# Attention's value product in three bursts instead of four, two heads folded at once by transposes, the end of the program joined to the last experts stage, and a batched comparison in the routing

## The chip, the cores and the metric

The program runs on one core of a Trainium2 chip. The time is that of one execution on the device, in microseconds (us); the median of several executions counts. TensorE (PE) multiplies matrices, VectorE (DVE), ScalarE (ACT) and GpSimd (POOL) work on rows, and SyncE (SP) mostly issues DMA transfers.

## What is computed

Four layers over 4 x 1024 tokens of 256 features, each with a residual and a layer norm: attention with 16 heads of 16 features, a dense mixture of the two best of 8 experts, a wavelet layer with linear attention, and a second mixture with capacity limits. Everything is fp32 at the interface.

```python
scores = jnp.einsum('bhqd,bhkd->bhqk', Q, K) * scale
attn = jax.nn.softmax(scores, axis=-1)
out = jnp.einsum('bhqk,bhkd->bhqd', attn, V)          # 64 heads of 1024 x 1024 in all
x = _layernorm(x + _L0_attn_ref(...)); x = _layernorm(x + _L0_ffn_ref(...))
x = _layernorm(x + _L1_attn_ref(...)); x = _layernorm(x + _L1_ffn_ref(...))
```

## The kernel before

The stages run one after the other, each in a block of its own; between blocks all engines meet, and GpSimd clears the stage's semaphores. Within a block each engine runs its own instruction list in program order, and semaphores order them among each other.

**Attention** (`stage_attention`) goes through the 64 heads (four per loop turn, u = 0 to 3). For each head and each of its 8 key tiles kt (128 keys), TensorE writes the transposed scores (128 keys x 1024 queries, two matmuls, L504) into one of two double banks `ps_scores`; ScalarE writes their exponential into `w` (L538; `w` is the name that the profile has for `c.probs`). The row maxima that the exponential needs are computed two heads ahead: each of 16 units per head is one matmul (L429) into a ring of three PSUM banks `ps_ring`, reduced by VectorE (L552). The ring also carries a small transpose per head (L437, "rows") and the fold. `claim(at)` makes TensorE wait until the bank is free again, that is, until unit at - 3 is used.

The value product (`pv`, L451) multiplies the padded values `v_padded` (32 columns: 16 values, a column of ones for the softmax sum, zeros) with the probabilities. It uses the array as four groups of 32 columns: j = 2 qh + kh, for two halves of the queries and the two key tiles of a pair. So the pair's four matmuls of 512 columns run side by side, and the sums over even and over odd key tiles stay apart in `ps_o`. A head has four such bursts: after key tile 3, 5, 7, and the last one after key tile 1 of the next head. ScalarE copies the bank (L527), and the *fold* (L461) turns it and adds even and odd key tiles by a matmul with a constant `fold`. VectorE then takes the reciprocal of the sum (L574) and multiplies (L576). An fp32 matmul is two instructions in the profile.

**Routing** (`stage_route`, run twice) ends with 64 outer products per run: VectorE makes a one-hot row of 128 (L1103, `e_oh_lo`) and a one-hot of the tile, 156 or 80 wide (L1104, `e_oh_hi`), and TensorE multiplies them (L1128), eight buffers deep.

**The end**: `stage_experts` (the second mixture) adds its rows to `sums` in memory by indirect DMAs of GpSimd (L1187) and waits for them. Then `stage_load_stats` loads `sums` into `y` in eight parts (L763) and takes statistics (L80), `stage_rstd` turns them into scale and shift by a chain of small operations (L789 to L803, the root on ScalarE at L809), and `stage_store` normalises on VectorE (L815) and stores in eight parts (L2065).

Of the kernel before, what the change touches and what calls it, by code (L numbers as in the profile page):

```python
# [19 lines left out]
E = 8  # L20
# [57 lines left out]
def row_stats(nc, c, i):  # L78

    nc.vector.bn_stats(c.six[:, bass.ds(i, 1), :].rearrange("p a d -> p (a d)"),  # L80
                       c.y[:, bass.ds(i, 1), :].rearrange("p a d -> p (a d)"))
# [17 lines left out]
def stage_constants(nc, mem, c):  # L99
# [3 lines left out]
    c.fold = mem.sb("fold", [P, 2 * 32])  # L103
    zeroed, made = mem.sem("consts_zeroed"), mem.sem("consts_made")
    with nc.Block() as block:
        @block.gpsimd
        def _(pool):
            nc.gpsimd.memset(c.ident[:, :], 0.0).then_inc(zeroed, 1)
            nc.gpsimd.memset(c.identb[:, :], 0.0).then_inc(zeroed, 1)
            nc.gpsimd.memset(c.fold[:, :], 0.0).then_inc(zeroed, 1)  # L110

            pool.wait_ge(zeroed, 3)
# [3 lines left out]

            fold = c.fold[:, :].rearrange("p (q r) -> p q r", q=2)
            for kh in range(2):

                pool.wait_ge(made, 2 + kh)  # L120
                nc.gpsimd.affine_select(out=fold, in_=fold, compare_op=ALU.not_equal, fill=1.0, base=-32 * kh,
                                        pattern=[[-64, 2], [-1, 32]], channel_multiplier=1).then_inc(made, 1)
# [142 lines left out]
def stage_attention(nc, a, c):  # L265
# [8 lines left out]
    with ExitStack() as stack:  # L274
# [5 lines left out]
        o_sb = mem.sb("o_transposed", [P, HALF])  # L280
# [5 lines left out]
        rec = mem.sb("o_reciprocal", [P, 2, 4])  # L286
# [17 lines left out]
        FOLD_AT, ROWS_AT = 4, 2  # L304

        def units(first, last, u):

            for kt in range(KT):
# [6 lines left out]
                if kt == FOLD_AT and not (first and u == 0):  # L315
                    yield kt, "fold"
# [10 lines left out]
        PER_GROUP = SLOTS * (2 * KT + 2)  # L327
        assert PER_GROUP % RING == 0

        def count_before(g, first, last, u):  # L330
# [4 lines left out]
            return g * PER_GROUP + (PROLOGUE - 1 + inside)  # L335

        def bank(g, first, last, u, j):
            base = PROLOGUE if first else PROLOGUE - 1
            return ring[(base + sum(len(list(units(first, last, w))) for w in range(u)) + j) % RING]
# [6 lines left out]
        with nc.Block() as block:  # L346
# [38 lines left out]
            def _(pool):  # L385
# [24 lines left out]
                def body(g, first, last):  # L410
                    for u in range(SLOTS):
                        n = g * SLOTS + u

                        wait_apart(pool, spare_p, pv_done, (n - 1) * 4)
# [7 lines left out]
            def _(pe):  # L422
# [18 lines left out]
                def pv(n, u, i):  # L441

                    pe.wait_ge(exp_done, n * KT + 2 * i + 2)
# [4 lines left out]
                    for kh in range(2):  # L448
# [27 lines left out]
                def body(g, first, last):  # L476
                    for u in range(SLOTS):
# [5 lines left out]
                        def emit(kt, kinds):  # L483
                            for j, (step, kind) in todo:
# [5 lines left out]
                                elif kind == "fold":  # L490
                                    fold_unit(n - 1, at, out)
                                else:
                                    max_unit((u + 2) % SLOTS, kt, int(kind[3]), at, out)
                        for kt in range(KT):
# [15 lines left out]
                            if kt == 1 and not (first and u == 0):  # L510
                                pv(n - 1, u + 1, KT // 2 - 1)
# [4 lines left out]
                pv(NH - 1, SLOTS - 1, KT // 2 - 1)  # L516
                end = count_before(GROUPS - 1, False, True, SLOTS)
                fold_unit(NH - 1, end, bank(GROUPS - 1, False, True, SLOTS, 0))

            @block.scalar  # L520
            def _(act):
                def copy_o(n, units_before):

                    act.wait_ge(pv_done, (n + 1) * (KT // 2))

                    act.wait_ge(ring_ready, units_before)
                    nc.scalar.activation(o_sb[:, :], p_o[:, :], ACT.Copy).then_inc(o_copied, 1)  # L527

                def body(g, first, last):
                    for u in range(SLOTS):  # L530
                        n = g * SLOTS + u
                        for kt in range(KT):

                            act.wait_ge(scores_ready, n * KT + kt + 1)
                            if kt % 2 == 0:

                                wait_from(act, pv_done, (n - 1) * (KT // 2) + kt // 2 + 1)
# [1679 lines left out]
```

## Time and profile before

| | us |
|---|---|
| median of 3 runs (range) | 2154.68 (2153.46 to 2157.82) |
| the profiled execution | 2156.69 |
| its span, first to last instruction | 2154.9 |
| TensorE busy | 1854.9 (86%) |
| VectorE busy | 1239.3 (58%) |
| ScalarE busy | 914.2 (42%) |
| GpSimd busy | 438.1 (20%) |

Busy times of a matmul include a modelled end, so neighbours overlap: a step is read from start to start. The granted clock is a share of full speed, 1.00 for 2.4 GHz and 0.50 for 1.2 GHz. "Idle before" names what an engine waited for.

### The profile page before, as it was taken

To read this page: it belongs to the slowest core of one execution; us is meant where nothing else is said; L and a number is where in the kernel's file an instruction comes from. 1 tells how busy PE (TensorE), PEld (TensorE's weight loads), DVE (VectorE), ACT (ScalarE), POOL (GpSimd) and SP (SyncE) were. 2 spreads that over 40 slices of the span, in tenths; PEclk is the share of its full clock that TensorE was granted. 3 is DMA by queue.
4 is the path that set the end of the run, shared out by engine and by line. 5 is a ranking of instruction groups with operands and counts; after the bars stand their busy time and mean duration, and the time that the engine had idled before them with its cause. 6 is when DMAs were issued, how large, how long until landed. Compare 5 with 4: busy or idle time off the path is not lost. (4 is left out here: it accounts for less than half of the span.)

```text
span 2154.9 us, 35159 instructions
## 1 busy us (share of the span) xinstructions
PE 1854.9 (86%) x9600; PEld 1119.4 (52%) x9601; DVE 1239.3 (58%) x2822; ACT 914.2 (42%) x1337; POOL 438.1 (20%) x573
## 2 busy tenths in 40 slices
PE   7899999999999999996599999999994885068771
PEld 4423333333333333363388888888884565037550
DVE  4588888888888888744711111111113796946335
ACT  3336666666666667753022233223331520031330
POOL 2210000000000000030023333333331001202771
PEclk9979999999999999998799999999997998586995
DMA  4511111111111111054433433443442001141224
GB/s 148 182 45 31 30 37 30 30 36 31 30 34 33 30 33 33 16 164 142 159 90 110 111 99 104 115 114 108 97 111 80 1 1 63 63 153 27 46 38 156
DMA packets 103317, 159.34 MB, mean 74 GB/s; under 512 B 20704, under 2 KB 79392, under 8 KB 97760
## 3 DMA queue, kind: packets, MB, share of 16 engines
q1 hardware_dynamic: 69712, 118.46, 16.9%
q0 software_dynamic: 22656, 24.51, 6.5%
q10 hardware_dynamic: 10896, 15.73, 2.1%
q8 instruction: 25, 0.41, 0.1%
q14 instruction: 28, 0.23, 0.0%
HBM read 124.19 MB, written 49.02 MB: 80 GB/s over the span
## 5 line engine op out<-in xcount | busy, mean ns | idle before, releaser
L552 DVE TENSOR_REDUCE unit_max<-ps_ring 128x1 f32<-128x512 f32 x1024 | 655.4, 686 | 83.7 <-PE ps_ring L429 73.4
L538 ACT ACTIVATE w<-ps_scores 128x1024 f32<-128x1024 f32 x512 | 510.0, 1023 | 266.2 <-PE ps_scores L504 254.4
L429 PE MATMUL ps_ring<-k_stack,q_stack 96*128 96x512 bf16 x1024 | 371.7, 391 | 9.8 <-POOL v_padded L392 9.2
L504 PE MATMUL ps_scores<-q_stack,k_stack 98*128 98x512 bf16 x1024 | 305.7, 380 | 0.1
L1495 PE MATMUL m_ps_h<-m_xt,m_w 128*128 128x256 f32 x1248 | 278.0, 381 | 0.8 <-DVE m_xt L1546 0.8
L1507 PE MATMUL m_ps_y<-w,m_ht 128*128 x1248 | 275.8, 379 | 0.0
L451 PE MATMUL ps_o<-w,v_padded 128*32 128x512 f32 x2048 | 272.8, 605 | 0.6 <-ACT w L538 0.6
L429 PEld LDWEIGHTS ps_ring<-k_stack,q_stack 96*128 96x128 bf16 x1024 | 102.1, 100 | 317.3 <-DVE unit_max L552 232.2
L1495 PEld LDWEIGHTS m_ps_h<-m_xt,m_w 128*128 128x128 f32 x1248 | 238.6, 191 | 34.0 <-DVE m_xt L1546 1.2
L1507 PEld LDWEIGHTS m_ps_y<-w,m_ht 128*128 128x128 f32 x1248 | 234.2, 190 | 30.3
L1527 ACT ACTIVATE m_ht<-m_ps_h,m_w 128x256 f32<-128x256 f32 x312 | 131.0, 471 | 143.7 <-PE m_ps_h L1495 143.7
L1546 DVE COPY m_xt<-m_ps_x 128x512 f32<-128x512 f32 x39 | 27.0, 692 | 276.2 <-PE m_ps_x L1483 276.2
L400 POOL TENSOR_SCALAR neg_max<-row_max 128x8 f32<-128x8 f32 x64 | 14.9, 233 | 707.0 <-DVE row_max L560 707.0
L1560 DVE TENSOR_TENSOR m_y<-m_ps_y,biases 128x256 f32<-128x256 f32 x78 | 33.1, 425 | 216.6 <-PE m_ps_y L1507 216.6
L1457 POOL DMA_INDIRECT sums<-m_y,m_is x78 | 124.6, 1597 | 143.9 <-ACT m_y L1532 131.2
L1532 ACT ACTIVATE m_y<-m_y,gains 128x256 f32<-128x256 f32 x78 | 39.6, 508 | 254.7 <-DVE m_y L1560 254.7
L504 PEld LDWEIGHTS ps_scores<-q_stack,k_stack 98*128 98x128 bf16 x1024 | 99.8, 98 | 79.9 <-issue 4.8
L1446 POOL DMA_INDIRECT m_x<-rows,m_ig x78 | 78.2, 1002 | 278.7 <-DVE m_ig L1542 265.8
L451 PEld LDWEIGHTS ps_o<-w,v_padded 128*32 128x32 f32 x2048 | 40.3, 107 | 107.2 <-issue 84.2
L880 PE MATMUL g_ps_t<-ident,g_rows 128*128 128x128 f32 x128 | 22.8, 309 | 79.3 <-DMA g_w<-in_gate 79.3
L1128 PE MATMUL e_ps_map<-e_oh_hi,e_oh_lo 128*128 128x156 f32 (+1 forms) x256 | 58.9, 393 | 22.2 <-DVE e_oh_hi L1104 22.2
L181 PE MATMUL ps_qk<-xt,w_qkv 128*128 128x512 f32 x128 | 58.5, 611 | 17.0 <-DMA bv_all<-in_bv 9.6
(230 smaller groups left out, 2008.9 us busy)
## 6 DMA issues: line engine op xcount, KB each, us to landing
m_w<-in_w SPq DMA_DIRECT2D x39, 1028.0 KB
rows<-g_rows SPq DMA_DIRECT2D x16, 512.0 KB, 2.9
y<-sums SPq DMA_DIRECT2D x16, 512.0 KB, 7.1
q_parts<-qk_part SPq DMA_DIRECT2D x16, 384.0 KB, 3.6
k_parts<-qk_part SPq DMA_DIRECT2D x16, 384.0 KB, 3.8
q_stack<-q_parts SPq DMA_DIRECT2D x64, 96.0 KB
k_stack<-k_parts SPq DMA_DIRECT2D x64, 96.0 KB
xt<-in_xt ACTq DMA_DIRECT2D x8, 512.0 KB, 4.2
```

The source lines that it names most:

```text
L181: mm = nc.tensor.matmul(pq[m][:, :], w[:, k, m * P:(m + 1) * P], xt[u][:, k, :], start=(k == 0), stop=(k == KC - 1))
L429: nc.tensor.matmul(out[:, :], qs[0:STACK, u, qt * P:(qt + 1) * P], ks[0:STACK, u, half * HALF:(half + 1) * HALF], start=True, stop=True).t ...
L451: mm = nc.tensor.matmul(p_o[32 * j:32 * j + 32, :], vpad[u % 2][:, 2 * i + kh, :], pt[:, 2 * i + kh, qh * HALF:(qh + 1) * HALF], start=(i ...
L504: mm = nc.tensor.matmul(p_s[kt % 2][:, half * HALF:(half + 1) * HALF], ks[:, u, kt * P:(kt + 1) * P], qs[:, u, half * HALF:(half + 1) * HALF],
L538: nc.scalar.activation(pt[:, kt, :], p_s[kt % 2][:, :], ACT.Exp, scale=SCALE)\
L552: nc.vector.tensor_reduce(unit_max[:, u % 2, half, qt:qt + 1], src[:, :], axis=AX.X, op=ALU.max).then_inc(ring_used, 1)
L1128: nc.tensor.matmul(p_m[:, 0:2 * tiles], oh_lo[u][:, :], oh_hi[u][:, :, :].rearrange("p a t -> p (a t)"), start=(first and u == 0), stop=(l ...
L1446: pool.indirect_dma_start(out=xg[u][:, j, :], out_offset=None, in_=rows, in_offset=bass.IndirectOffsetOnAxis(ap=ig[u][j][:, :], axis=0))\
L1457: pool.indirect_dma_start(out=sums, out_offset=bass.IndirectOffsetOnAxis(ap=isc[u][j][:, :], axis=0), in_=ys[u][:, j, :], in_offset=None, ...
L1495: mm = nc.tensor.matmul(p_h[f // 2][:, f % 2 * T:(f % 2 + 1) * T], w1s[u][:, at:at + P], xt[u][:, k, :], start=(k == 0), stop=(k == KC - 1))
L1507: mm = nc.tensor.matmul(p_y[j][:, 0:D], ht[u][:, f, j * P:(j + 1) * P], w2[:, bass.ds(e * FC + f, 1), :].rearrange("p a d -> p (a d)"), st ...
L1527: nc.scalar.activation(ht[u][:, f, :], p_h[f // 2][:, f % 2 * T:(f % 2 + 1) * T], func, bias=w1s[u][:, KC * F + f:KC * F + f + 1]).then_in ...
```

## The change

In attention the four column groups now belong to four quarters of the queries (blocks of 128 queries, j of each half), so each key tile makes one group of four matmuls of 256 columns, and all 8 key tiles add up in place. The bursts hold key tiles 0 to 2, 3 to 5 and 6 to 7 and stand after key tile 4, 7, and 1 of the next head. `ps_o` has 256 columns; ScalarE copies them (L527 before) into one half of `o_transposed`, and once in two heads TensorE transposes the four blocks of 128 with the identity. That unit counts as two in the ring ("spare" and "fold") but uses one bank. VectorE's reciprocal and multiply then serve two heads.

In the routing, eight low one-hots are made by one comparison. The end no longer has stages of its own: a new class `Finish` adds its instructions to the lists of the experts stage, in two halves, with the rows shared by ScalarE and VectorE. The constant `fold` is gone.

```diff
-        FOLD_AT, ROWS_AT = 4, 2
+        FOLD_AT, ROWS_AT, COPY_AT = 4, 2, 1
+        EDGES = (0, 3, 6, KT)
+        BURSTS = len(EDGES) - 1
...
-                if kt == FOLD_AT and not (first and u == 0):
+                if kt == FOLD_AT and u % 2 == 0 and not (first and u == 0):
+                    yield kt, "spare"
                     yield kt, "fold"
...
                 def pv(n, u, i):
-                    pe.wait_ge(exp_done, n * KT + 2 * i + 2)
+                    pe.wait_ge(exp_done, n * KT + EDGES[i + 1])
...
-                    for kh in range(2):
-                        for qh in range(2):
-                            j = 2 * qh + kh
-                            mm = nc.tensor.matmul(p_o[32 * j:32 * j + 32, :], vpad[u % 2][:, 2 * i + kh, :],
-                                                  pt[:, 2 * i + kh, qh * HALF:(qh + 1) * HALF],
-                                                  start=(i == 0), stop=(i == KT // 2 - 1))
+                    for kt in range(EDGES[i], EDGES[i + 1]):
+                        probs = pt[:, kt, :].rearrange("p (b j q) -> p j b q", b=2, j=4)
+                        for j in range(4):
+                            mm = nc.tensor.matmul(p_o[32 * j:32 * j + 32, 0:2 * P], vpad[u % 2][:, kt, :],
+                                                  probs[:, j, :, :], start=(kt == 0), stop=(kt == KT - 1))
                     mm.then_inc(pv_done, 1)
...
-                    pe.wait_ge(o_copied, n + 1)
-                    claim(at)
+                    pe.wait_ge(o_copied, n + 2)
+                    claim(at + 1)
                     for blk in range(4):
-                        mm = nc.tensor.matmul(out[:, blk * 64:(blk + 1) * 64], o_sb[:, blk * P:(blk + 1) * P],
-                                              c.fold[:, :], start=True, stop=True)
-                    mm.then_inc(ring_ready, 1)
+                        mm = nc.tensor.transpose(out[:, blk * P:(blk + 1) * P],
+                                                 o_sb[:, blk // 2, blk % 2 * P:(blk % 2 + 1) * P], c.ident[:, :])
+                        if blk >= 2:
+                            mm.then_inc(ring_ready, 1)
...
-                            if kt in (3, 5, 7):
-                                pv(n, u, (kt - 3) // 2)
+                            if kt in (4, 7):
+                                pv(n, u, (kt - 4) // 3)
...
-                        v.tensor_scalar(oh_lo[u][:, :], iota_p[:, :], lo[:, k, bass.ds(i, 1)], None, ALU.is_equal)
+                        if at == 0:
+                            wait_from(dve, mapped, g * (2 * DEEP) + (h - 1) * DEEP)
+                            shape = [P, 2, DEEP // 2, P]
+                            v.tensor_tensor(oh_lo[h][:, :, :, :],
+                                            bcast(iota_p[:, :].unsqueeze(1).unsqueeze(1), shape),
+                                            bcast(lo[:, :, bass.ds(i0, DEEP // 2)].unsqueeze(3), shape), ALU.is_equal)
...
+            if finish is not None:
+                @block.sync
+                def _(sp):
+                    for u in range(2):
+                        sp.wait_ge(added[u], 8 * tiles)
+                    finish.loads_and_stores(sp)
...
+    def statistics(self, dve):
+        for half in range(2):
+            for h in range(4 * half, 4 * half + 4):
+                dve.wait_ge(self.loaded[h], 16)
+                for i in range(h * self.EACH, (h + 1) * self.EACH):
+                    last = row_stats(nc, c, i)
...
+        for h in (4, 5):
+            for i in range(h * self.EACH, (h + 1) * self.EACH):
+                last = normalised(nc, c, self.rows[:, i, :], i)
+            last.then_inc(self.dve_rows, 1)
+    def roots_and_rows(self, act):
+        for half in range(2):
+            act.wait_ge(self.var_ready, half + 1)
+            nc.scalar.activation(self.root[:, cut], self.var[:, cut], ACT.Sqrt).then_inc(self.root_ready, 1)
+            act.wait_ge(self.scale_ready, half + 1)
+            for h in ((0, 1, 2, 3), (6, 7))[half]:
+                for i in range(h * self.EACH, (h + 1) * self.EACH):
+                    last = nc.scalar.activation(self.rows[:, i, :], c.y[:, i, :], ACT.Identity,
+                                                scale=c.rstd[:, i:i + 1], bias=c.nmr[:, i:i + 1])
+                last.then_inc(self.act_rows, 1)
```

On TensorE, around the fold in the loop over heads, the list before reads as follows (`ps_o` marks a burst of the value product, `ps_ring` with stacks a maximum, with `o_transposed` the fold; the count is that of matmuls as written, each fp32 one being two instructions):

```order
L429 MATMUL ps_ring<-k_stack,q_stack 128x512
L451 MATMUL ps_o<-w,v_padded 32x512 x4
L429 MATMUL ps_ring<-k_stack,q_stack 128x512
L504 MATMUL ps_scores<-q_stack,k_stack 128x512 x2
L429 MATMUL ps_ring<-k_stack,q_stack 128x512
L461 MATMUL ps_ring<-fold,o_transposed 128x64 x4
L429 MATMUL ps_ring<-k_stack,q_stack 128x512
L504 MATMUL ps_scores<-q_stack,k_stack 128x512 x2
L429 MATMUL ps_ring<-k_stack,q_stack 128x512
L451 MATMUL ps_o<-w,v_padded 32x512 x4
```

and the list of the changed kernel at the same place, once in two heads:

```order
L423 MATMUL ps_ring<-k_stack,q_stack 128x512
L445 MATMUL ps_o<-w,v_padded 32x256 x12
L454 MATMUL ps_ring<-ident,o_transposed 128x128 x4
L423 MATMUL ps_ring<-k_stack,q_stack 128x512
L500 MATMUL ps_scores<-q_stack,k_stack 128x512 x2
L423 MATMUL ps_ring<-k_stack,q_stack 128x512 x2
L500 MATMUL ps_scores<-q_stack,k_stack 128x512 x2
L423 MATMUL ps_ring<-k_stack,q_stack 128x512 x2
L500 MATMUL ps_scores<-q_stack,k_stack 128x512 x2
L423 MATMUL ps_ring<-k_stack,q_stack 128x512
L445 MATMUL ps_o<-w,v_padded 32x256 x12
```

The fold has moved from the middle of a stretch between two bursts to right behind a burst, and three key tiles instead of two stand between the bursts. On ScalarE, at the end of the program, the list before ends with the root:

```order
L1299 ACTIVATE m_y_1<-m_y_1,gains 128x256 x2
L1169 UNCONDITIONAL_BRANCH
L806 UNCONDITIONAL_BRANCH
L809 ACT_TABLE_LOAD
L809 ACTIVATE r_root<-r_var 128x32
```

and that of the changed kernel has rows behind each of two roots:

```order
L1313 ACTIVATE m_y_1<-m_y_1,gains 128x256 x2
L2141 ACT_TABLE_LOAD
L2141 ACTIVATE f_root<-f_var 128x16
L2146 ACTIVATE f_rows<-y,nmr,rstd 128x256 x16
L2141 ACTIVATE f_root<-f_var 128x16
L2146 ACTIVATE f_rows<-y,nmr,rstd 128x256 x8
```

The second root stands behind 16 rows, and the branches from block to block are gone.

## Rows read from the trace of the kernel before

**Rows 1.** Timeline of GpSimd at the start: start, duration, engine, line, operation, count.

```profile
2.17 0.63 POOL L121 TENSOR_SCALAR_AFFINE_SELECT fold<-fold 128x64 f32<-128x64 f32 x2
```

**Rows 2.** Table of stretches: stretch, length, busy of each engine, granted clock, DMA share.

```profile
200.00:800.00 600.00, 600.00 (x3508) 211.81 (x3504) 526.32 (x961) 411.44 (x433) 44.05 (x192) 1.00 0.11 32
```

**Rows 3.** Timeline of TensorE over one head.

```profile
501.06 1.00 PE L461 MATMUL ps_ring<-fold,o_transposed 128*128 128x64 f32 x8
501.90 0.38 PE L429 MATMUL ps_ring<-k_stack,q_stack 96*128 96x512 bf16 x1
502.12 0.59 PE L504 MATMUL ps_scores<-q_stack,k_stack 98*128 98x512 bf16 x2
502.55 0.38 PE L429 MATMUL ps_ring<-k_stack,q_stack 96*128 96x512 bf16 x1
502.86 1.07 PE L451 MATMUL ps_o<-w,v_padded 128*32 128x512 f32 x8
503.86 0.39 PE L429 MATMUL ps_ring<-k_stack,q_stack 96*128 96x512 bf16 x1
...
513.56 1.00 PE L461 MATMUL ps_ring<-fold,o_transposed 128*128 128x64 f32 x8
```

**Rows 4.** The first four matmuls of that burst, its loads, and durations min/median/max (ns).

```profile
502.86 0.64 PE L451 MATMUL ps_o<-w,v_padded 128*32 128x512 f32 x4
502.86 0.16 PEld L451 LDWEIGHTS ps_o<-w,v_padded 128*32 128x32 f32 x8 [0.42 <-issue]
L451 PE MATMUL ps_o<-w,v_padded x2048: 589/593/617, 137.4 to 925.7; 128*32 128x512 f32 x187
```

**Rows 5.** Waits from 200 to 800 us: total, times, longest.

```profile
DVE unit_max L552 <- PE ps_ring L429: 49.6, 144, 0.5
```

**Rows 6.** Timeline of VectorE in the same head.

```profile
502.10 0.21 DVE L574 RECIPROCAL o_reciprocal<-ps_ring 128x8 f32<-128x8 f32 x1
...
502.66 1.28 DVE L552 TENSOR_REDUCE unit_max<-ps_ring 128x1 f32<-128x512 f32 x2
504.29 2.54 DVE L552 TENSOR_REDUCE unit_max<-ps_ring 128x1 f32<-128x512 f32 x4 [0.35 <-PE ps_ring L429]
```

**Rows 7.** Timeline of TensorE in the first experts stage.

```profile
1244.49 1.46 PE L1495 MATMUL m_ps_h<-m_xt,m_w 128*128 128x256 f32 x6
1245.78 0.60 PE L1483 MATMUL m_ps_x<-ident,m_x 128*128 128x128 f32 x4
```

**Rows 8.** Routing: VectorE's timeline, the second routing's stretch, a group of VectorE.

```profile
1060.41 0.27 DVE L1103 TENSOR_SCALAR e_oh_lo<-e_iota_p,e_lo 128x128 f32<-128x128 f32 x1
1060.61 0.37 DVE L1104 SCALAR_TENSOR_TENSOR e_oh_hi<-e_iota_t,e_hi,e_value 128x156 f32<-128x156 f32 x1
...
1941.00:1968.50 27.50, 27.27 (x128) 27.28 (x128) 25.90 (x127) 0.00 (x0) 0.00 (x0) 0.50 0.00 1
...
L1041 DVE TENSOR_TENSOR e_pr<-e_ex,e_rc 128x256 f32<-128x256 f32 x2 | 0.8, 425 | 0.1
```

**Rows 9.** The end: GpSimd's drain and clears, a ScalarE group, the timeline.

```profile
L1169 POOLq DRAIN  x1: 3937/3937/3937, 2115.6 to 2115.6; - x1
L46 POOLq EVENT_SEMAPHORE_RANGE_CLEAR  x31: 37/38/43, 2119.8 to 2140.8; - x31
L1299 ACT ACTIVATE m_y<-m_y,gains 128x256 f32<-128x256 f32 x40 | 20.3, 508 | 74.0 <-DVE m_y L1367 69.6 <-issue 4.3
2119.80 7.86 SPq L763 DMA_DIRECT2D y<-sums  x8
2127.47 5.54 DVE L80 BATCH_NORM_STATS2 six<-y 128x6 f32<-128x256 f32 x16 [1.14 <-DMA y<-sums]
...
2136.80 0.21 DVE L789 TENSOR_TENSOR mean<-six 128x32 f32<-128x32 f32 x1 [0.30 <-PEq L759]
...
2140.73 10.43 DVE L815 TENSOR_SCALAR s_rows<-y,rstd,nmr 128x256 f32<-128x256 f32 x32 [0.56 <-PEq L784]
2142.14 9.42 SPq L2065 DMA_DIRECT2D out_rows<-s_rows  x8
```

More of the change, by code:

```diff
@@ L109, in _ @@
             nc.gpsimd.memset(c.identb[:, :], 0.0).then_inc(zeroed, 1)
-            nc.gpsimd.memset(c.fold[:, :], 0.0).then_inc(zeroed, 1)
-            pool.wait_ge(zeroed, 3)
+            pool.wait_ge(zeroed, 2)
             for m in (c.ident, c.identb):
@@ L534, in body @@
                             act.wait_ge(scores_ready, n * KT + kt + 1)
[L535 to L537 removed]
+                            if kt in EDGES:
+                                wait_from(act, pv_done, (n - 1) * BURSTS + EDGES.index(kt) + 1)
                             nc.scalar.activation(pt[:, kt, :], p_s[kt % 2][:, :], ACT.Exp, scale=SCALE)\
                                 .then_inc(exp_done, 1)
[L540 to L541 removed]
+                            if kt == COPY_AT and not (first and u == 0):
+                                copy_o(n - 1, u + 1, count_before(g, first, last, u))
                 groups(act, body)
[L543 removed]
+                copy_o(NH - 1, SLOTS - 1, count_before(GROUPS - 1, False, True, SLOTS))
             @block.vector
@@ L604, in _ @@
                 end = count_before(GROUPS - 1, False, True, SLOTS)
-                normalise(NH - 1, end, bank(GROUPS - 1, False, True, SLOTS, 0))
+                normalise(NH - 2, NH // 2 - 1, end, bank(GROUPS - 1, False, True, SLOTS, 1))
         mem.clear()
@@ L972, in stage_route @@
         ownf = mem.sb("e_ownf", [P, owners])
-        oh_lo = [mem.sb(f"e_oh_lo{u}", [P, P]) for u in range(DEEP)]
-        oh_hi = [mem.sb(f"e_oh_hi{u}", [P, 2, tiles]) for u in range(DEEP)]
+        oh_lo = [mem.sb(f"e_oh_lo{h}", [P, 2, DEEP // 2, P]) for h in range(2)]
+        oh_hi = [mem.sb(f"e_oh_hi{u}", [P, 2, tiles]) for u in range(2 * DEEP)]
         table = mem.sb("e_table", [P, 2, tiles])
@@ L1125, in outer_products, with stage_experts @@
                 def outer_products(g, first, last):
-                    for u in range(DEEP):
-                        pe.wait_ge(hi_done, g * DEEP + u + 1)
-                        nc.tensor.matmul(p_m[:, 0:2 * tiles], oh_lo[u][:, :],
+                    for u in range(2 * DEEP):
+                        pe.wait_ge(hi_done, g * (2 * DEEP) + u + 1)
+                        nc.tensor.matmul(p_m[:, 0:2 * tiles], oh_lo[u // DEEP][:, u % 2, u % DEEP // 2, :],
                                          oh_hi[u][:, :, :].rearrange("p a t -> p (a t)"),
-                                         start=(first and u == 0), stop=(last and u == DEEP - 1)).then_inc(mapped, 1)
-                peeled_ends(pe, 2 * NT // DEEP, outer_products)
+                                         start=(first and u == 0), stop=(last and u == 2 * DEEP - 1)).then_inc(mapped, 1)
+                peeled_ends(pe, NT // DEEP, outer_products)
         mem.clear()
-def stage_experts(nc, c, tiles, fixed, F, w1, w2, b1, b2, func, rows, sums):
+def stage_experts(nc, c, tiles, fixed, F, w1, w2, b1, b2, func, rows, sums, finish=None):
     FC = F // P
@@ L1215, in _ @@
                 add(tiles - 1, 1)
-                for u in range(2):
-                    pool.wait_ge(added[u], 8 * tiles)
+                if finish is None:
+                    for u in range(2):
+                        pool.wait_ge(added[u], 8 * tiles)
+            if finish is not None:
+                @block.sync
+                def _(sp):
+                    for u in range(2):
+                        sp.wait_ge(added[u], 8 * tiles)
+                    finish.loads_and_stores(sp)
             @block.tensor
@@ L1323, in _ @@
                 scale_y(tiles - 1, 1)
+                if finish is not None:
+                    finish.roots_and_rows(act)
             @block.vector
@@ L1385, in _ @@
                 bias_y(tiles - 1, 1, expert(tiles // STEP - 1, STEP - 1))
+                if finish is not None:
+                    finish.statistics(dve)
         mem.clear()
@@ L2173, in _ @@
                     dve.wait_ge(loaded, 64)
-            stage_experts(nc, c, CAP * E, CAP, D, w1, w2, b1, b2, ACT.Silu, rows[1], sums[1])
-            stage_load_stats(nc, c, sums[1])
-            stage_rstd(nc, c)
-            stage_store(nc, c, out)
+            finish = Finish(nc, c, m, sums[1], out)
+            stage_experts(nc, c, CAP * E, CAP, D, w1, w2, b1, b2, ACT.Silu, rows[1], sums[1], finish)
 def kernel(**inputs):
```

149 lines of the change are left out of this document (91 added, 58 removed).

## Prediction

> **What bounds the kernel now.** The first loads wait for the constants, and the two selects of the fold's constant take 0.63 us of that [rows 1]; that is small. I read the table of stretches first, since the change touches four places far apart. From 200 to 800 us TensorE is busy in all of the 600 us, at a granted clock of 1.00, VectorE in 526 and ScalarE in 411 of them [rows 2]. So attention, some 800 us long, looks bound by TensorE. Its timeline confirms it, and gives the prices. The fold of one head starts at 501.06 and that of the next at 513.56 [rows 3]: 12.50 us a head. In between, one maximum matmul takes 0.22 us (501.90 to 502.12), a key tile's two score matmuls 0.43 (502.12 to 502.55), the fold 0.84 (501.06 to 501.90), and from the maximum matmul at 502.55 to the one behind the burst at 503.86 it is 1.31, so a burst of two key tiles costs 1.31 - 0.22 = 1.09 us. Four column groups run side by side in a burst. It is two passes of four instructions: the union of the first four is 0.64 us long [rows 4], that of all eight 1.07 [rows 3], so a pass streams for 0.43. Two passes are 0.86, and 1.09 - 0.86 = 0.23 us is the price of going into a burst and out of it. A head's sum: 16 maxima 3.5, 8 score pairs 3.5, 4 bursts 4.36, fold 0.84, the row unit with its waits about 0.3: 12.5. Nothing is left over.
>
> VectorE is close behind. It waits for TensorE's maxima 49.6 us in the 48 heads of that stretch [rows 5], 1.03 us a head, one wait of 0.35 behind most bursts; its own work is thus 12.50 - 1.03 = 11.47. Four reductions in a row last 2.54 us [rows 6], one every 0.62.
>
> **The change, part by part.** *Fold.* Now eight instructions a head (four fp32 matmuls); then four fp32 transposes for two heads. Four such transposes in another stage have a union of 0.60 us [rows 7]; the fold's union is 1.00 and costs 0.84 [rows 3], so I take 0.16 off here too: 0.44 us, 0.22 a head. That is 0.84 - 0.22 = 0.62 saved per head.
>
> *Bursts.* Three a head for four saves one entry and exit: 0.23.
>
> *Passes.* Each key tile now has two passes of 256 columns, 16 a head for 8 of 512. Six fp32 instructions of 256 columns take 1.29 us from 1244.49 to 1245.78 [rows 7], 0.215 each, so 16 x 0.215 = 3.44, against 8 x 0.43 = 3.44: nothing, if the passes follow each other like that. This is the one large unknown. One matmul of the second pass lasts 0.593 and one of the first 0.617 [rows 4]; the union of four is 0.64, so the groups start spread over 0.02. The second pass then starts at 1.07 - 0.593 - 0.02 = 0.457 behind the first, 0.025 more than a pass streams. That can be the load of the first weights (once a burst) or the spread of the four groups (then every pass may pay it). I take once, since the two unions differ by only 0.43; the other bound is all 16 passes, 16 x 0.025 = 0.4 us a head. The Trainium skill, "TensorE: Matmul & The Clock Gate", Part 3 (speedup against the span model), puts a packed group at one matmul's time plus some 4 ns for each further tile; paid by every pass that would be an estimated 16 x 12 ns = 0.2 us a head, halfway, and the trace so far does not tell at which passes it is paid.
>
> *VectorE.* Reciprocal, its wait and the multiply stand between 502.10 and 502.66, 0.56 us, [rows 6] once a head; then once for two heads, with a multiply of 256 elements for one of 128, about 0.7. It saves 0.2 a head, off the path.
>
> *Ring.* This takes some back. Stretches between bursts grow from two key tiles to three. TensorE issues six maxima in 2.6 us, VectorE needs 6 x 0.62 = 3.7, and there are three banks. By hand, with 0.43 us from a maximum's start to its reduction's (503.86 to 504.29 [rows 3, 6]), a reduction's 0.68 (2.54 - 3 x 0.62) and 0.07 more until its bank is reused, the fifth maximum waits 0.07 in a plain stretch. Behind the fold it is worse: its unit counts as two, so for a moment two banks are left, and VectorE starts 0.7 us late. There the third maximum waits 0.17 and the fifth 0.35, 0.52 for two heads. Together 0.35 us a head. The lower bound is the present one, 0.06; the upper one, if the fold's stretch stalls twice as long and plain ones 0.2, is 0.8.
>
> Sum for attention: -0.62 - 0.23 + 0 + 0.35 = -0.50, with a few hundredths for the gaps: -0.48 a head, 64 x 0.48 = **-31 us**. ScalarE has 411 of 600 us busy and its copy halves; the exponentials that a burst needs were already awaited by the scores before it, so neither adds.
>
> *Routing.* VectorE's low one-hot lasts 0.27 us and the high one starts 0.20 behind it, so neighbours overlap by 0.07; the high one lasts 0.37, a step of 0.29 to 0.30 [rows 8]. A pair is 0.49. A batched comparison has 1024 elements. A tensor-tensor of 256 takes 0.425 [rows 8] and a reduction of 512 about 0.69 [rows 6], 1.02 ns an element, so 1.21, or 1.15 a step. Eight pairs: 1.15 + 8 x 0.29 = 3.47 for 3.90; 64 pairs save 8 x 0.43 = 3.4 us, as long as TensorE keeps up. In the second routing it doesn't: from 1941 to 1968.5 it is busy in 27.3 of 27.5 us at a granted clock of 0.50 (1.2 GHz), and VectorE in 25.9 [rows 8]. There the saving is nothing, and the first matmul comes 0.9 us later, behind the long comparison. Net **-2.5**, between -8 (the second at 2.4 GHz) and +2 (the first at 1.2).
>
> *End.* Once the last scatter has landed, GpSimd drains for 3.94 us from 2115.6 on, and only at 2119.80 do the loads go out [rows 9]. SyncE, in the same block and with a wait of its own for the scatter, skips 4.2 us. From the load issue on I count anew. Half of the rows have their statistics at 2127.47 + 5.54/2 = 2130.2, +10.4. The small chain, now 2136.80 to 2140.73 with a block change (3.9), should take about 3.1: scale at +13.5. ScalarE's row of 256 with a per-partition gain takes 0.51 [rows 9], about 0.40 a step: 16 rows to +19.9. VectorE's second statistics end at +19.0, its chain near +22.1 (the root queues behind ScalarE's rows). The last 16 rows, eight on each engine (VectorE 0.33 each), end near +25.3. The four last stores hold the DMA engines 1.37 us each from about +24.7 (eight went between the first issue at 2142.14 and the end at 2154.9, 12.8 us, of which I leave 0.9 in front and 0.9 behind), so +30.1, and the end +30.9. Behind the block stand twenty semaphore clears of GpSimd of 0.038 us each [rows 9]; with gaps of the same order 1.3: +32.2. Now it is 2154.9 - 2119.8 = 35.1. That is -2.9 - 4.2 = **-7**; the bounds are -11 (clears at nothing, ScalarE's rows at 0.33 as VectorE's) and -3 (its rows at the full 0.51).
>
> *Constants.* Without the fold's memset and two selects (0.63 us for the selects [rows 1], 0.8 with the waits around them) the first loads go out **0.8** earlier.
>
> The sum: -31 - 2.5 - 7 - 0.8 = -41 us. The profiled span 2154.9 becomes 2113.6; its execution took 2156.7, 2.0 above the median of 2154.7, so the median comes to **2113**.
>
> **The rivals.**
> (a) Every pass pays the groups' stagger: 16 x 0.025 = 0.4 a head, 25 us back: 2138. For it: the spread of 0.02 is as large as what the second pass is late. Against it: the unions. Chance 0.27.
> (b) The ring stalls at its upper bound, 0.45 us a head more: 29 us back, 2142. VectorE's waits would stay above 1 us a head. Chance 0.08.
> (c) The other side: weights. Now both passes' eight loads go out at the start of a burst (a union of 0.16 us for all eight [rows 4]); a third set needs the place that the first holds. If sets three to six (ten a head) lay bare, at the 0.11 us that a load takes (0.16 less the spread of eight issues), that is +1.1 a head: +0.62 x 64 = +40, less the 10 of the other parts, 2185. It decides from 0.50/10 = 0.05 us a pass on. Against it: full-array loads here are issued while the matmul before them streams. Chance 0.04. The Trainium skill, same page, Part 3 (what overlaps), says that a weight load overlaps running matmuls only where its row group differs; the four groups here share all rows, and by that rule the time would be this one. What the trace shows of second passes speaks against it.
> (d) VectorE becomes the bound: if the two long bursts add their whole extra pass pair, 0.43 each, to its wait, it has 11.47 - 0.2 + 3 x 0.35 + 0.86 = 13.2 us a head, +43 us less 10: 2187. It needs waits over 1.2 us a head. Against it: six reductions (3.7) in a stretch and burst of 4.1 on TensorE leave 0.4 idle, not more. Chance 0.02.
>
> **How the numbers follow.** My forecast has 0.55, its own range 2104 to 2124 (ring 0.2 to 0.5, the end and routing by their bounds); (a) 0.27, (b) 0.08, (c) and (d) 0.06, and 0.04 for a granted clock that falls differently in the small stages (as in the second routing, 0.50 [rows 8]; 27 us at this level, of which the matmuls would need half). The range 2104 to 2142 holds forecast and (a). A measurement here tells 0.2%, 4 us, from no change: faster 0.93, same 0.02, slower 0.05.
>
> **What would show it.** Right: 12.0 us from head to head; the first pass of a burst to the third in 0.43 to 0.44 us; transposes 0.44 a pair of heads; VectorE's waits for maxima near 1 us a head and new waits of TensorE on VectorE after the fold; loads of the last stage issued within 0.3 us of the last landing. Wrong: 0.24 us from pass to pass (a), 0.32 (c), or waits on the ring at every stretch (b).

## The result, and the profile after

| | us |
|---|---|
| changed kernel, median of 4 runs | 2126.27 (2125.93 to 2127.73) |
| kernel before, median of 4 runs beside it | 2154.42 (2153.46 to 2157.82) |
| ratio, 95% interval | 0.9866 (0.9854 to 0.9878) |
| span of the profiled execution | 2125.9, before 2154.9 |

It is faster by 28 us, where 41 were forecast. The time is 2 us outside the forecast's own range (2104 to 2124). It is inside the full range (2104 to 2142) only because that one holds rival (a) as well, and the bursts below don't behave as (a) has it; so that it fell inside is luck. The first line of the page's busy times, and the table of stretches from 200 to 800 us (length, then busy us and count for TensorE, its weight loads, VectorE, ScalarE and GpSimd; then clock, DMA share, GB/s):

```profile
PE 1809.8 (85%) x11264; PEld 1147.6 (54%) x11265; DVE 1201.9 (57%) x2635; ACT 905.9 (43%) x1362; POOL 436.5 (21%) x570
...
200.00:800.00 600.00, 590.53 (x4896) 242.69 (x4894) 523.91 (x941) 408.80 (x446) 44.59 (x196) 1.00 0.12 33
```

TensorE no longer fills the stretch as in [rows 2]. The period of a head is read from ScalarE's copies of `ps_o`, one a head (duration min/median/max, first and last start):

```profile
L523 ACT ACTIVATE o_transposed<-ps_o x45: 383/383/383, 210.1 to 743.5; 128x256 f32<-128x256 f32 x45
```

44 steps in 533.4 us are 12.12 us a head; before they are 12.50. All periods below are read so. TensorE's timeline over the transposes and two bursts, with the weight loads (PEld) of the first:

```profile
505.48 0.66 PE L454 MATMUL ps_ring<-ident,o_transposed 128*128 128x128 f32 x4
505.97 0.38 PE L423 MATMUL ps_ring<-k_stack,q_stack 96*128 96x512 bf16 x1
...
506.62 0.38 PE L423 MATMUL ps_ring<-k_stack,q_stack 96*128 96x512 bf16 x1
507.25 0.39 PE L423 MATMUL ps_ring<-k_stack,q_stack 96*128 96x512 bf16 x1 [0.25 <-DVE biases L573]
...
507.91 0.38 PE L423 MATMUL ps_ring<-k_stack,q_stack 96*128 96x512 bf16 x1
508.45 0.39 PE L423 MATMUL ps_ring<-k_stack,q_stack 96*128 96x512 bf16 x1 [0.15 <-DVE unit_max L548]
...
509.11 0.38 PE L423 MATMUL ps_ring<-k_stack,q_stack 96*128 96x512 bf16 x1
509.42 1.50 PE L445 MATMUL ps_o<-w,v_padded 128*32 128x256 f32 x24
509.42 1.02 PEld L445 LDWEIGHTS ps_o<-w,v_padded 128*32 128x32 f32 x24 [0.28 <-ACT w L534]
510.85 0.39 PE L423 MATMUL ps_ring<-k_stack,q_stack 96*128 96x512 bf16 x1
...
512.38 0.38 PE L423 MATMUL ps_ring<-k_stack,q_stack 96*128 96x512 bf16 x1
512.69 1.07 PE L445 MATMUL ps_o<-w,v_padded 128*32 128x256 f32 x16
513.69 0.39 PE L423 MATMUL ps_ring<-k_stack,q_stack 96*128 96x512 bf16 x1
```

The burst of three key tiles takes 510.85 - 509.11 - 0.22 = 1.52 us and that of two 1.09. The transposes take 0.49 a pair of heads, in place of two folds of 0.84 [rows 3]. But a maximum without a wait is 0.22 behind the one before, and 507.25 and 508.45 stand 0.63 and 0.54 behind: 0.41 and 0.32 late. They are the third and the fifth maximum behind the transposes. VectorE beside it, and its part in the waits from 200 to 800 us (total, times, longest):

```profile
502.32 3.08 DVE L548 TENSOR_REDUCE unit_max<-ps_ring 128x1 f32<-128x512 f32 x5
506.17 0.26 DVE L570 RECIPROCAL o_reciprocal<-ps_ring 128x16 f32<-128x16 f32 x1 [0.76 <-PE ps_ring L454]
506.77 0.42 DVE L573 TENSOR_TENSOR biases<-ps_ring,o_reciprocal 128x256 f32 x1 [0.34 <-DVE o_reciprocal L570]
507.11 2.47 DVE L548 TENSOR_REDUCE unit_max<-ps_ring 128x1 f32<-128x512 f32 x4
```

```profile
DVE unit_max L548 <- PE ps_ring L423: 42.6, 123, 0.5
DVE o_reciprocal L570 <- PE ps_ring L454: 19.1, 25, 0.8
PEld ps_ring L423 <- DVE biases L573: 14.7, 25, 0.9
PE ps_ring L423 <- DVE biases L573: 5.6, 25, 0.5
```

VectorE has read every maximum by 505.40, near the end of the burst, and waits 0.76 us for the transposes. Then come reciprocal, increment and multiply, 1.02 us until 507.19, and only the end of the multiply frees the bank of the transposes. The routings, by VectorE's timeline, and the second by the table of stretches:

```profile
1015.49 1.23 DVE L1106 TENSOR_TENSOR e_oh_lo<-e_iota_p,e_lo 128x1024 f32<-128x1024 f32 x1
...
1043.96 0.32 DVE L1117 COPY e_table<-e_ps_map 128x156 f32<-128x156 f32 x1 [0.62 <-PE e_ps_map L1133]
...
1916.38 1.22 DVE L1106 TENSOR_TENSOR e_oh_lo<-e_iota_p,e_lo 128x1024 f32<-128x1024 f32 x1
...
1945.50 0.24 DVE L1117 COPY e_table<-e_ps_map 128x80 f32<-128x80 f32 x1 [3.90 <-PE e_ps_map L1133]
```

```profile
1917.00:1944.50 27.50, 26.63 (x125) 26.63 (x126) 22.61 (x72) 0.00 (x0) 0.00 (x0) 0.50 0.00 1
```

From the first low one-hot to the copy of the table: 28.5 us in the first (before 31.9), 29.1 in the second (before 28.2). The end, by the timeline:

```profile
2092.88 8.48 SPq L2087 DMA_DIRECT2D y<-sums  x8
...
2101.17 2.77 DVE L80 BATCH_NORM_STATS2 six<-y 128x6 f32<-128x256 f32 x8 [1.76 <-DMA y<-sums]
...
2106.54 7.97 ACT L2146 ACTIVATE f_rows<-y,nmr,rstd 128x256 f32<-128x256 f32 x16 [1.37 <-DVE nmr L2128]
2108.64 11.78 SPq L2090 DMA_DIRECT2D out_rows<-f_rows  x8
...
2114.65 0.25 DVE L2123 RECIPROCAL rstd<-f_root 128x16 f32<-128x16 f32 x1 [1.92 <-ACT f_root L2141]
...
2115.99 2.67 DVE L814 TENSOR_SCALAR f_rows<-y,rstd,nmr 128x256 f32<-128x256 f32 x8
2115.99 4.04 ACT L2146 ACTIVATE f_rows<-y,nmr,rstd 128x256 f32<-128x256 f32 x8 [1.36 <-DVE nmr L2128]
```

The loads go out 2.78 us behind the last scatter's issue (before 7.13), and from there to the end are 33.0 us (before 35.1).

### The profile page after: what moved, and what is told of

It is laid out like the page before. It is cut to its first block and busy times, and to the rows that moved or that the text cites. A ratio compares the mean times of both kernels' runs of the same rounds, so it can differ in the third digit from the quotient of the medians.

```text
span 2125.9 us, 37885 instructions
## 1 busy us (share of the span) xinstructions
PE 1809.8 (85%) x11264; PEld 1147.6 (54%) x11265; DVE 1201.9 (57%) x2635; ACT 905.9 (43%) x1362; POOL 436.5 (21%) x570
## 5 line engine op out<-in xcount | busy, mean ns | idle before, releaser
L548 DVE TENSOR_REDUCE unit_max<-ps_ring 128x1 f32<-128x512 f32 x1024 | 639.6, 684 | 70.5 <-PE ps_ring L423 64.4
L534 ACT ACTIVATE w<-ps_scores 128x1024 f32<-128x1024 f32 x512 | 503.6, 1022 | 265.4 <-PE ps_scores L500 262.7
L445 PE MATMUL ps_o<-w,v_padded 128*32 128x256 f32 x4096 | 260.8, 384 | 0.0
L445 PEld LDWEIGHTS ps_o<-w,v_padded 128*32 128x32 f32 x4096 | 113.4, 109 | 119.1 <-issue 53.0
L1133 PE MATMUL e_ps_map<-e_oh_hi,e_oh_lo 128*128 128x156 f32 (+1 forms) x256 | 50.0, 379 | 28.5 <-DVE e_oh_hi L1109 28.5
```

The costliest lines, as they stand in the source:

```text
L445: mm = nc.tensor.matmul(p_o[32 * j:32 * j + 32, 0:2 * P], vpad[u % 2][:, kt, :], probs[:, j, :, :], start=(kt == 0), stop=(kt == KT - 1))
L534: nc.scalar.activation(pt[:, kt, :], p_s[kt % 2][:, :], ACT.Exp, scale=SCALE)\
L548: nc.vector.tensor_reduce(unit_max[:, u % 2, half, qt:qt + 1], src[:, :], axis=AX.X, op=ALU.max).then_inc(ring_used, 1)
L1133: nc.tensor.matmul(p_m[:, 0:2 * tiles], oh_lo[u // DEEP][:, u % 2, u % DEEP // 2, :], oh_hi[u][:, :, :].rearrange("p a t -> p (a t)"), sta ...
```

## The experiments

All times are medians; the kernel before, run beside each, lay between 2154.6 and 2156.6. "Period" is us per head.

| run | us | ratio, 95% | period |
|---|---|---|---|
| e1 attention's change alone | 2132.6 | 0.9877 to 0.9910 | 12.12 |
| e2 four bursts | 2123.0 | 0.9834 to 0.9867 | 12.155 |
| e3 transposes at key tile 6 | 2127.2 | 0.9845 to 0.9882 | 12.16 |
| e4 increment first | 2119.6 | 0.9805 to 0.9847 | 12.04 |
| e5 = e2 + e4 | 2123.2 | 0.9840 to 0.9887 | 12.155 |
| e6 after, half reductions | 2098.7 | 0.9720 to 0.9752 | 11.81 |
| e7 before, half reductions | 2143.0 | 0.9932 to 0.9968 | 12.44 |
| e8 the end alone | 2152.1 | 0.9971 to 0.9990 | 12.50 |
| e9 empty place apart | 2120.2 | 0.9823 to 0.9853 | 12.08 |
| e10 = e6 + e4 | 2089.4 | 0.9676 to 0.9705 | 11.735 |
| e11 the routing alone | 2153.5 | 0.9978 to 0.9997 | 12.50 |
| e12 transposes ahead of the burst | 2106.4 | 0.9759 to 0.9788 | 11.85 |

**e1.** All hunks of `stage_attention`, on the kernel before.

> The kernel before with only the attention part of the change (value product, fold, copies); routing, end and constants as before. If the ledger of the two traces holds (first score to last normalised head: 796.5 us before, 775.0 after), this gives 2154.4 - 21.5 = 2133 us, within 3. If part of the gain of attention was only the clock or the order of stages, it lies above 2138; the prediction on record would have had it at 2123.

2132.6: attention brings 22 of the 28 us, with the same period as in the changed kernel.

**e2.** On the changed kernel:

```diff
-        EDGES = (0, 3, 6, KT)
+        EDGES = (0, 2, 4, 6, KT)
...
-                            if kt in (4, 7):
-                                pv(n, u, (kt - 4) // 3)
+                            if kt in (3, 5, 7):
+                                pv(n, u, (kt - 3) // 2)
```

> The changed kernel with the old four bursts of two key tiles (after key tiles 3, 5, 7 and 1 of the next head), fold in pairs kept, which then stands in the middle of a stretch again. One more entry and exit costs 0.23 us a head, 15 us in all. Theory A (the ring stalls because the fold stands right behind a burst): the stall behind the fold, 0.73 us for two heads, mostly goes, so the net is +0 to +5 us, 2126 to 2131. Rival B (long stretches as such stall the ring): the stalls of all stretches go, net -5 or better, 2121 or less. Rival C (the stalls are the same anywhere): +15, 2141.

2123.0, between theory A and rival B, and the total misleads. The period is 0.035 us longer. From the first copy to the last this makes only 0.7 us, since the last three steps, whose heads have few maxima or none, are 1.6 us shorter. The span is 4.5 us shorter all the same, by 1.2 up to the first copy, 2.2 in the stages behind attention and 1.9 behind the last scatter. By the period it is theory A. So the burst edge that the change saves, 0.23 on TensorE's list, is given back almost whole in waits. TensorE now waits in front of the transposes:

```profile
505.23 0.42 PEld L454 LDWEIGHTS ps_ring<-ident,o_transposed 128*128 128x128 f32 x4 [0.63 <-DVE unit_max L548]
505.23 0.66 PE L454 MATMUL ps_ring<-ident,o_transposed 128*128 128x128 f32 x4
505.93 0.26 DVE L570 RECIPROCAL o_reciprocal<-ps_ring 128x16 f32<-128x16 f32 x1
```

The maximum before starts at 504.72, so the transposes are 0.3 us late. VectorE no longer idles ahead of the reciprocal.

**e3.** `FOLD_AT` from 4 to 6: the transposes in the middle of a stretch.

> The changed kernel with the fold's unit moved from key tile 4 (right behind a burst) to key tile 6, into the middle of the next stretch, one key tile before the following burst. Theory A: the waits behind the fold fall from 0.73 to about 0.3 us for two heads, 32 x 0.45 = 14 us faster, 2112. Rival B (the stall belongs to the stretch of three key tiles and only moves): within 3 us of the changed kernel's 2126.

2127.2 and a longer period, rival B: the stall only moves, in front of the transposes.

```profile
508.15 0.65 PE L454 MATMUL ps_ring<-ident,o_transposed 128*128 128x128 f32 x4 [0.52 <-DVE unit_max L548]
```

**e4.** The increment for the empty place of the ring, until now between reciprocal and multiply, goes ahead:

```diff
-                    dve.wait_ge(ring_ready, at + 2)
                     wait_from(dve, ring_used, at)
+                    nc.vector.sem_inc(ring_used, 1)
+                    dve.wait_ge(ring_ready, at + 2)
                     ...
                     dve.wait_ge(rec_done, pair + 1)
-                    nc.vector.sem_inc(ring_used, 1)
```

> The changed kernel with VectorE's increment for the spare unit put before the reciprocal, where it is already true, not between reciprocal and multiply. The multiply now starts 0.60 us behind the reciprocal's start; before it was 0.35. Theory A: this 0.25 us stands in TensorE's wait for the multiply once for two heads, 32 x 0.25 = 8 us faster, 2118. Rival: the wait for the next reduction grows by as much, no change within 2 us.

2119.6, as theory A has it; the period falls by 0.08. TensorE behind the transposes, and VectorE:

```profile
502.66 0.38 PE L423 MATMUL ps_ring<-k_stack,q_stack 96*128 96x512 bf16 x1
503.31 0.82 PE L423 MATMUL ps_ring<-k_stack,q_stack 96*128 96x512 bf16 x2
...
502.86 0.26 DVE L570 RECIPROCAL o_reciprocal<-ps_ring 128x16 f32<-128x16 f32 x1 [0.76 <-PE ps_ring L454]
503.26 0.42 DVE L572 TENSOR_TENSOR biases<-ps_ring,o_reciprocal 128x256 f32 x1
```

The row of two maxima holds the second and the third. The third starts at 503.31 + 0.82 - 0.38 = 503.75, so it is 0.22 late, where it was 0.41 late without this edit. The multiply starts 0.40 us behind the reciprocal instead of 0.60, and VectorE's waits between them fall from 7.9 us in 25 to 1.9 in 12 (200 to 800 us). The wait of 0.76 is as before.

**e5.** Both edits, e2 and e4.

> Value product in four bursts of two key tiles (as in the four-burst run) and the increment ahead of the wait and the reciprocal (as in the run with the increment first). Theory A, the two gains are of different stalls (one behind each long stretch, one behind the fold): 2123.0 - 6.7 = 2116, and the multiply 0.35 to 0.40 us behind the reciprocal. Rival B, both relieve the same lateness of VectorE, and the second gains nothing more: within 2 us of the better alone, 2118 to 2121. Rival C, four bursts leave VectorE too little slack in front of the fold for the increment to matter: 2123.

Rival C: the same period as e2. There the late step is the wait ahead of the transposes, which the increment doesn't shorten.

**e6, e7.** In the changed kernel and in the kernel before, each reduction takes half of its columns, so half of the scores are left out of the maxima:

```diff
-  nc.vector.tensor_reduce(unit_max[...], src[:, :], axis=AX.X, op=ALU.max)
+  nc.vector.tensor_reduce(unit_max[...], src[:, 0:256], axis=AX.X, op=ALU.max)
```

> The changed kernel with each of VectorE's reductions over 256 of its 512 columns (half of the scores are left out of the maxima), so that one takes about 0.43 us instead of 0.69; TensorE's list is the same. By starts of its rows TensorE's own list is 16 maxima at 0.22, 8 scores at 0.43, bursts of 1.52, 1.52 and 1.09, half of 0.49 and about 0.15 for the rows, together 11.5 us a head, while a head takes 12.14. Theory A, the missing 0.65 is all waiting for VectorE's ring: 64 x 0.65 = 41 us less, 2085, and waits of TensorE on the ring near nothing. Rival B, about half of it is the ring, the rest is other lateness (ScalarE's exponentials, changes of mode): 2106. Rival C, VectorE's lateness is not what costs: above 2120.

> The kernel before with the same shortened reductions (half of the scores left out of the maxima). Its list by the same count is 3.52 + 3.44 + 4 x 1.09 + 0.84 + 0.15 = 12.3 us a head, for 12.50. Theory A: it waits little on the ring, 0.2 a head: 2154.5 - 13 = 2141 or more, so that with shortened reductions the change is worth 41 - 13 + 28 = 56 us instead of 28. Rival B: before waits as much as after (0.5 or more a head): 2122 or less, and VectorE's share in the missed forecast is nothing.

ScalarE's copies in e6 and e7:

```profile
L523 ACT ACTIVATE o_transposed<-ps_o x45: 384/384/384, 213.1 to 732.8; 128x256 f32<-128x256 f32 x45
```

```profile
L527 ACT ACTIVATE o_transposed<-ps_o x45: 597/597/598, 214.2 to 761.7; 128x512 f32<-128x512 f32 x45
```

The period falls by 0.31 after the change and by 0.06 before it. So e7 bears out theory A, and e6 lies at rival B: the reductions' length explains 0.25 us a head of the difference between the two kernels, and of the time over TensorE's list (11.5 us) 0.3 stays. The totals hold more than this. The first score comes 5.7 us earlier in e7 and 3.8 in e6 (against the changed kernel): the first maxima, ahead of the heads, get shorter too, and the clock is back sooner. From 120 to 130 us it is 1.00 in e7 and 0.79 in e6, and 0.50 in both kernels with full reductions.

**e10.** e6 with the increment first.

> Reductions over half of the columns (half of the scores left out of the maxima) and the increment first. Theory A: of the 0.3 us a head by which 11.81 still stands above TensorE's own list of 11.5, the increment between reciprocal and multiply (0.25 us per two heads) is 0.12: 11.69 a head, 2098.7 - 8 = 2091. Rival B: with short reductions VectorE waits for TensorE anyway, the increment is hidden: 11.8 a head, 2098. Rival C: the whole 0.3 is the chain behind the transposes, and goes: 11.5, 2079.

11.735, a fall of 0.08 as in e4 with full reductions, so the increment costs the same whether or not VectorE has time; theory A expected 0.12. That its total of 2091 came nearly true is luck, for the first copy comes 4.2 us earlier than in e6. Some 0.2 over the list remains, and these runs don't split it.

**e9.** On e4: the empty place of the ring moves from in front of the transposes to behind the last maximum of the head, whose matmul and reduction increment by two.

```diff
                 if kt == FOLD_AT and u % 2 == 0 and not (first and u == 0):
-                    yield kt, "spare"
                     yield kt, "fold"
+                if kt == KT - 1 and u % 2 == 0 and not (first and u == 0):
+                    yield kt, "spare"
...
-                    claim(at + 1)
+                    claim(at)
```

> The changed kernel with three bursts, but the empty place of the ring ("spare") no longer stands in front of the transposes: it stands behind the last maximum of the head, ahead of the burst, where VectorE has caught up, and is counted by that maximum and its reduction (both increment by two), so that no increment of its own is left. The transposes then wait for one reduction less. With the increment first a head takes 12.04 us, and VectorE still idles 0.76 us in front of each reciprocal. Theory A: the transposes run under the last reduction, the idle time falls to about 0.35, 0.4 us per two heads: 12.04 - 0.2 = 11.84 a head, 2119.6 - 13 = 2107. Rival B: the third maximum behind the transposes waits for the multiply as before, the lateness only moves: 12.0 or more a head, 2117 to 2120. Rival C: the empty place costs as much where it now stands: 2122 or more.

Rival B, and 0.04 a head more than e4, as the multiply stands 0.50 behind the reciprocal here. The transposes start no earlier, since it wasn't the ring that held them but the burst ahead of them:

```profile
500.37 1.50 PE L446 MATMUL ps_o<-w,v_padded 128*32 128x256 f32 x24
501.80 0.66 PE L455 MATMUL ps_ring<-ident,o_transposed 128*128 128x128 f32 x4
...
502.50 0.26 DVE L571 RECIPROCAL o_reciprocal<-ps_ring 128x16 f32<-128x16 f32 x1 [0.77 <-PE ps_ring L455]
```

**e12.** On e9, the transposes go between the scores and the last maximum of key tile 4, ahead of the burst:

```diff
-                            emit(kt, ("rows", "max1"))
+                            emit(kt, ("fold", "rows", "max1"))
...
-                            emit(kt, ("fold",))
```

> As the run with the empty place apart, and the four transposes are issued ahead of the last maximum of key tile 4, in front of the burst instead of right behind it. Theory A: what costs behind the burst is that VectorE has read every maximum by its end and idles 0.77 us for transposes and reciprocal, and that reciprocal and multiply (0.84 us) then fall into the stretch. Ahead of the burst it still has maxima to read when the transposes run, and the burst of 1.52 us covers reciprocal and multiply: 0.3 to 0.5 us less per two heads, 12.07 becomes 11.85 a head, 2120 - 13 = 2107. Rival B: the lateness only moves, since the transposes now wait for a reduction ahead of the burst (as they did at key tile 6): 12.05 to 12.2 a head, 2119 to 2127. Rival C: somewhere between, 11.95, 2113.

2106.4 us, 50 less than before and 20 less than the changed kernel: theory A. The timelines of TensorE and VectorE:

```profile
517.86 0.60 PE L455 MATMUL ps_ring<-ident,o_transposed 128*128 128x128 f32 x4
...
518.39 0.39 PE L424 MATMUL ps_ring<-k_stack,q_stack 96*128 96x512 bf16 x1
...
518.71 1.50 PE L446 MATMUL ps_o<-w,v_padded 128*32 128x256 f32 x24
519.04 0.26 DVE L570 RECIPROCAL o_reciprocal<-ps_ring 128x16 f32<-128x16 f32 x1
519.46 0.42 DVE L572 TENSOR_TENSOR biases<-ps_ring,o_reciprocal 128x256 f32 x1 [0.16 <-DVE o_reciprocal L570]
```

VectorE is still reading maxima when the transposes run, so its 0.76 us of idle time is gone, and reciprocal and multiply lie under the burst.

**e8.** The kernel before with `Finish` and what calls it, nothing else.

> The kernel before with the end joined to the last experts stage and nothing else. Theory A, the end is worth what the milestones of the changed kernel say, last scatter to end 42.3 before and 35.8 after, so -6.4: 2148. Rival B, the end is worth the forecast -7 or more and the changed kernel loses some of it elsewhere: 2146 or less. Rival C, the experts stage pays for the added instructions (code of three engines more): 2151 or more.

By its total, -3.6, it is rival C, but not by its mechanism: from the last copy to the last scatter, where the added instructions would cost, it takes 0.4 us more than before. And from the last scatter's issue to the end it takes 7.6 us less than before, the forecast size. It had lost 3.6 us ahead of the last scatter, nearly all of it early: 0.6 to the first maximum, 2.7 from there to the first copy, in instructions that are those of the kernel before. The table of stretches shows the clock there, for before, e8 and the changed kernel in turn:

```profile
130.00:140.00 10.00, 9.85 (x36) 2.98 (x35) 8.96 (x17) 4.79 (x5) 0.86 (x4) 0.73 0.04 10
140.00:150.00 10.00, 10.00 (x59) 2.72 (x57) 9.12 (x17) 7.75 (x9) 0.86 (x4) 1.00 0.15 41
```

```profile
130.00:140.00 10.00, 9.92 (x25) 2.65 (x28) 8.55 (x16) 4.04 (x4) 0.86 (x4) 0.50 0.05 17
140.00:150.00 10.00, 10.00 (x56) 2.68 (x48) 7.56 (x14) 5.70 (x7) 0.86 (x4) 0.89 0.11 33
```

```profile
130.00:140.00 10.00, 9.92 (x23) 2.89 (x24) 8.56 (x16) 3.75 (x4) 0.85 (x4) 0.50 0.07 21
140.00:150.00 10.00, 10.00 (x88) 3.81 (x86) 7.92 (x14) 6.15 (x7) 0.85 (x4) 0.91 0.15 41
```

With 1.00 and 0.50 as the two levels, full speed returns at about 135.4, 142.2 and 141.8 us.

**e11.** The kernel before with the batched comparison alone.

> The kernel before with the batched comparison of the routing and nothing else. Theory A, by the milestones of the changed kernel: first routing (first low one-hot to the copy of the table) 31.92 to 28.5 us, second 28.2 to 29.1: -2.5, 2152. Rival B: the second routing finds its clock at full speed and gains as the first does: 2148. Rival C: nothing in the time, since the granted clock of the stages behind it falls otherwise: 2154 or more, with the two routings themselves as in A.

Its parts are those of theory A (first routing -3.5, second +0.9); its total is -2.3 with an interval that nearly reaches no change, and its profiled span only 0.5 shorter, since this execution stood at +1.6 by the first maximum.

## Why the prediction was right in sign and 13 us off in size

By its own steps; spans are 2154.9 and 2125.9, so -29.0 for a forecast of -41.3. Of the 12 us between them attention is 7.7, what lies in front of its heads 3.9, and the end 0.6.

*Bursts and passes: right.* A burst of three key tiles costs 1.52 us and one of two 1.09, so two passes cost 0.43, 0.215 each, and 0.23 is paid once. Rivals (a) and (c) wanted 0.24 or 0.32 a pass, 1.67 us and more a burst. The rule of the Trainium skill ("TensorE: Matmul & The Clock Gate", Part 3) that a weight load overlaps a running matmul only in another row group would have given (c); here 24 loads of column groups that share all rows lie inside the 1.50 us of their matmuls (a union of 1.02), so the trace disagrees with the rule.

*Transposes: nearly right.* 0.49 for a forecast of 0.44 a pair.

*The ring stall: the step that failed in size.* The forecast took 0.35 us a head from bounds of 0.06 and 0.8. TensorE's list became shorter by 0.84 - 0.49 / 2 = 0.60 and by 0.23, nearly the forecast 0.85, but the period by 0.38, so the stall is 0.45, and attention between the first and the last copy gave 23.3 us (779.3 to 756.0) for 31.

The timeline shows which wait was too small. Behind the transposes the fifth maximum was forecast 0.35 late and is 0.32 late. The third was forecast 0.17 late and is 0.41 late: 0.24 for two heads or 0.12 a head, as much as the whole miss of 0.10. It waits for the multiply, and here the prediction's "about 0.7" for reciprocal, wait and multiply is what failed: until the next reduction starts they take 0.94 (506.17 to 507.11). It had left out the increment between them. With the increment first (e4) the third maximum is 0.22 late, the three steps take 0.74, and the period falls by 0.08, as it does in e10.

The prediction had seen that VectorE would be late there, but took the place as given. Right behind a burst VectorE has run out of work; it waits 0.76 us for the transposes, while TensorE goes on filling the ring. e12 moves the transposes and takes 0.23 a head away. That the reductions' length carries 0.25 of the stall is shown by e6 and e7; how the 0.12 that these and the increment leave is to be divided stays open. Rival (b) asked for waits of VectorE above 1 us a head. Its waits for maxima are 42.6 us in 49.5 heads, 0.86, and 1.25 with those for the transposes, so its sign is there only if both count; the stall itself, 0.45, is far from its 0.8.

*In front of the heads: not in the forecast.* The loads go out 0.87 us earlier, for 0.8. But the first maximum is 0.9 us later than before. That is scatter as far as these runs show: at 113.2 us it lies between the 111.5 (e10) and 115.2 (e6) of kernels whose instructions up to there are the same. And from there to the first copy it takes 37.0 us for 34.8, because the clock returns later: e1, with the same attention and the clock back at about 137 (0.65 from 130 to 140 us), needs 34.8. Together 3.1 us later at the first copy, for 0.8 earlier. The prediction gave a differently falling clock 0.04 and no size. e8 shows that this happens with the same instructions, and e5, whose clock is back at 135.4 like that of before, needs 34.8. What decides the return is open.

*Routing: right*, -3.5 and +0.9 for -3.4 and +0.9.

*The end: right in parts.* Earlier loads gave 4.35 for 4.2. The rest gave 2.1 for 2.9: ScalarE's rows step by 0.50 us instead of the 0.40 assumed (16 rows: 7.97 us), and by +21.6 instead of +19.9 they hold the second root back 1.9 us. The upper bound of [rows 9], 0.51, would have been the value to take. From the last scatter on it is 6.5 us in all, and 6.2 to 8.3 in the other kernels with the same end (e2 to e5, e8, e9, e12). This spread is the landing of the loads: in the first half of the statistics VectorE waits 1.76 us for them in the changed kernel, 2.06 in e9, 1.45 in e12, 0.69 in e8 and nothing in e2 and e4, and from the last scatter to the end these take 35.8, 36.1, 35.5, 34.7 and 34.0 us.

*The small stages between* sum to +0.1.

## What to carry to other kernels

When a change shortens the list of the engine that bounds a kernel, ask at each new place what the engine that empties its buffers is doing there: work that needs a round trip between both (transpose, then normalise) belongs ahead of a long burst, while the other engine still has something to read, and not behind it. Serial steps that hold a shared ring are priced by where they stand; an increment of a semaphore between two dependent instructions counts as one of them. And on this kernel read a variant's gain from its period or its milestones: totals of variants differ by 3 us through the clock and the first 100 us alone, and by 2 more through the last loads.

## What the runs showed of the hardware

From reciprocal to multiply, which wait on each other through a semaphore, VectorE took 0.60 us with an increment between them, 0.40 with it ahead of both (e4), 0.42 and 0.50 without any (e12, e9); before, 0.35 on half the elements in the fold's shape. So the increment isn't all that sets this gap; the rest is unexplained. The return of TensorE's clock from 0.50 to 1.00 (1.2 to 2.4 GHz) in front of the same instructions came at 135.4 us in one execution and at 142.2 in another program's, and was worth 2.7 us. The same eight loads at the end of the program made VectorE wait between nothing (e2, e4) and 2.06 us (e9). A matmul and a reduction can each increment their semaphore by two (e9, e12), which saved the increment.
